# A gated graph network on one core: the update gate next to the reset gate in the first of a round's six steps

## The reference

```
h = relu(layernorm(x));  q, k, v = h@Wq.T, h@Wk.T, h@Wv.T
rel = adj.T * (q@k.T);   rel /= norm(rel, axis=2);   x = x + rel@v
h = relu(layernorm(x))
repeat 3 times:
    a = adj@h (used as a_in and as a_out);  av = [a, a]
    z = sigmoid(av@w3.T + b3 + h@u3.T + bu3)
    r = sigmoid(av@w4.T + b4 + h@u3.T + bu3)
    c = tanh  (av@w5.T + b5 + (r*h)@u5.T + bu5)
    h = (1-z)*h + z*c
x = x + h
```

## Time and profile before

| | |
|---|---|
| median of 3 runs | 1028.66 us (1027.58 to 1029.11) |
| span of the profiled execution | 1027.9 us (no device time of its own is listed for it) |
| PE busy | 990.2 us, 96% |
| DVE busy | 773.5 us, 75% |
| ACT busy | 596.1 us, 58% |
| POOL busy | 87.3 us, 8% |
| mean granted TensorE clock | 0.991 |

### The profile page before, as it was taken

How to read it: one execution, slowest core, us unless ns; L and a number is a source line. 1 busy time by engine, 2 the same in 40 slices (tenths; PEclk the granted TensorE clock), 3 DMA queues, 4 the chain that set the end, 5 groups by cost and what they waited for, 6 DMA issues and landing times.

```text
span 1027.9 us, 16089 instructions
## 1 busy us (share of the span) xinstructions
PE 990.2 (96%) x5448; PEld 852.0 (83%) x5448; DVE 773.5 (75%) x1519; ACT 596.1 (58%) x1050; POOL 87.3 (8%) x90
## 2 busy tenths in 40 slices
PE   5799999999999999999999999999999999999996
PEld 4778888888888888878888788887888888888885
DVE  4877768778687777877778776877868777687765
ACT  4546665566656575665656556556564566655562
POOL 1110001001011010100001000100001000010000
PEclk9799999999999999999999999999999999999999
DMA  5010000200001000100002000010000100000001
GB/s 160 2 41 1 1 1 21 63 0 0 0 20 62 0 0 0 58 25 0 0 0 82 1 0 0 20 62 0 0 0 20 62 0 0 0 20 21 1 2 41
DMA packets 21409, 20.32 MB, mean 20 GB/s; under 512 B 2160, under 2 KB 21360, under 8 KB 21360
## 3 DMA queue, kind: packets, MB, share of 16 engines
q1 hardware_dynamic: 21360, 19.83, 6.1%
HBM read 11.44 MB, written 8.39 MB: 19 GB/s over the span
## 4 chain that ended last, share of the span: by engine, by line
PE 88%; DVE 5%; issue 3%; ACT 3%; DMA 1%; DVEq 0%; SPq 0%; POOL 0%; ACTq 0%
PE gate L304 12%; PE gate L306 11%; PE gate L305 11%; PE cand L304 8%; PE cand L306 8%; PE cand L305 8%; PE tok L395 3%; PE fea L405 3%; PE tok L405 3%; PE tok L304 2%; PE tok L306 2%; PE tok L305 2%; PE fea L360 2%; PE fea L304 1%; PE fea L306 1%
## 5 line engine op out<-in xcount | busy, mean ns | idle before, releaser
L854 DVE TENSOR_TENSOR d_s<-c_s,h 128x512 f32<-128x512 f32 x96 | 64.2, 688 | 58.6 <-ACT c_s L694 43.7
L675 ACT ACTIVATE r_s<-gate,b_r 128x512 f32<-128x512 f32 x96 | 64.2, 684 | 75.3 <-PE gate L306 75.3
L597 ACT ACTIVATE h_hi<-h 128x512 fp32r<-128x512 f32 x64 | 39.5, 632 | 98.6 <-DVE h L991 98.6
L264 POOL TENSOR_TENSOR rstd<-vare,minus_half 128x4 f32<-128x4 f32 x32 | 38.2, 1194 | 517.1 <-DVE vare L882 517.1
L304 PE MATMUL gate<-a_hi,W_hi_wz 128*128 128x512 f32 x192 | 79.3, 413 | 0.4
L597 ACT ACTIVATE a_hi<-a_s 128x512 fp32r<-128x512 f32 x96 | 60.5, 630 | 31.6 <-DVE a_s L958 31.1
L694 ACT ACTIVATE c_s<-cand,b_c 128x512 f32<-128x512 f32 x96 | 64.7, 682 | 22.8 <-PE cand L306 20.8
L304 PE MATMUL cand<-a_hi,W_hi_w 128*128 128x512 f32 x192 | 77.9, 406 | 0.0
L304 PE MATMUL cand<-rh_hi,W_hi_u 128*128 128x512 f32 x192 | 77.5, 404 | 0.0
L304 PE MATMUL gate<-h_hi,W_hi_u 128*128 128x512 f32 x192 | 76.3, 397 | 0.0
L305 PE MATMUL gate<-h_lo,W_hi_u 128*128 128x512 f32 x192 | 75.5, 393 | 0.0
(11 more groups left out here) (129 smaller groups left out, 2709.8 us busy)
## 6 DMA issues: line engine op xcount, KB each, us to landing
x_s<-x SPq DMA_DIRECT2D x16, 512.0 KB, 4.8
out<-o_s SPq DMA_DIRECT2D x16, 512.0 KB, 3.0
z_s<-w_t SPq DMA_DIRECT2D x1, 512.0 KB, 4.1
r_s<-w_t SPq DMA_DIRECT2D x1, 512.0 KB, 4.9
c_s<-w_t SPq DMA_DIRECT2D x1, 512.0 KB, 5.9
rh<-u_t SPq DMA_DIRECT2D x2, 256.0 KB, 6.2
d_s<-wq SPq DMA_DIRECT2D x1, 256.0 KB, 3.8
d_s<-wk SPq DMA_DIRECT2D x1, 256.0 KB, 4.6
```

The lines of the kernel that those rows point to most:

```text
L264: nc.gpsimd.tensor_tensor(rstd[n][:], vare[n][:], minus_half[:], ALU.pow).then_inc(rstd_ready[n], 1)
L597: return nc.scalar.activation(dst, src, ACT.Copy)
L675: nc.scalar.activation(r_s[:, c, :], gate[:, c, :], ACT.Sigmoid, bias=b_r[:, c:c + 1]).then_inc(r_ready, 1)
L854: return nc.vector.tensor_tensor(dst, a, b, ALU.subtract)
```

## The change

Only the order of work in window 1 changes, on three engines. On PE the update gate comes directly behind the reset gate, then the transposes, then `candidate_a`, and then both adjacency products next to each other. On ACT the reset sigmoid comes ahead of the state's copies, and the copy of r*h ahead of that of the transposed state. On DVE the low half of r*h comes ahead of the first adjacency sum (and so ahead of `shifts`). No instruction is added or removed.

```diff
@@ tensor, window, k == 1
                     reset_gate(w, s)
+                    update_gate(w, s)
                     transpose_state(w, o, use("step 1"))
-                    update_gate(w, s)
+                    candidate_a(w, s)
                     pe.wait_ge(tok_taken, 2 * use("step 1") + 2)
                     adjacency(w + 1, 0, feaA, use("adj 1"))
-                    candidate_a(w, s)
                     adjacency(w + 1, 1, tokA, use("adj' 1"))
                     candidate_rh(w, s)
@@ scalar, window, k == 1
+                    reset_sigmoid(w)
                     split_state(w, o)
-                    reset_sigmoid(w)
+                    split_rh(w)
                     split_tok(use("step 1"))
                     update_sigmoid(w)
                     take_a_aside(0, feaA, use("adj 1"))
-                    split_rh(w)
                     if attention:
                         normalise(0, 2 * i + 2, 0)
                     take_a_aside(1, tokA, use("adj' 1"))
```

## The result

The changed kernel takes 1040.67 us (median of 4, 1040.32 to 1041.73) against 1028.80 in the same comparison: ratio 1.0118, 95% interval 1.0104 to 1.0132. It is slower by 1.2%, as forecast (1039 us, range 1031 to 1044). One disturbed execution of a kernel further down (1114.15 us, at a mean granted clock of 0.847) is left out of all figures.

A forecast was written before the change was run, and what follows sets the result against it. PE, busy 990.2 of 1027.9 us, was taken to bound the kernel. Six rounds at +1.4 (8.4), +1.6 in the first and +0.1 behind the loop make +10.1, so 1039 us, range 1031 to 1044.

The forecast's parts named there:

- The pause that goes: Window 1, PE behind the reset gate: two pauses, 1.33 us together, vanish; with 0.14 of change-overs a gift of 1.47 us each round.
- The chain behind it: Window 1, ACT and DVE: later copies put `candidate_rh` 0.25 us later than before and `transpose_hx` 1.56 us late.
- What comes back in window 2: PE's existing 0.68 us wait for `a_s` shrinks, so 1.4 us a round stays of 1.56; bounds 0.25 and 1.56.
- The sum: Whole program: 8.4 us for rounds 2 to 7, 1.6 first round, 0.1 behind the loop: +10.1, median 1039 us.
- ACT's own turn of the loop: ACT's loop top: a costlier turn makes the second sigmoid 0.63 us later, +3.8 more, 1042.6 us; chance 0.08.
- that rival: PE's clock: window 1's two pauses bring half clock for 6.5 us each round, +23, 1062 us; chance 0.07.
- Faster: Window 1: DVE doesn't bind, PE keeps its 1.47 us a round, -10.3, 1018.4 us; chance 0.06.
- little changes: Window 1: `candidate_rh` waits as forecast, the wait ahead of `transpose_hx` is hidden, +0.25 x 7, 1030.4 us; chance 0.09.
- a granted clock under 0.99: Sign on PE's clock, listed among those that would show the prediction wrong.

The follow-up runs named there:

- one swap ahead of each wait: Against the changed kernel, separately: r*h ahead of `h_lo` on DVE, 1031.31 us; second `take_a_aside` ahead of the layer norm (`hx`) on ACT, 1032.12 us.
- both with the shifts: Changed kernel with r*h ahead of `h_lo`, second `take_a_aside` ahead of `hx`, and `shifts` ahead of `sum_a(0)`: 1023.05 us, ratio 0.9935.
- two kernels: PE's new order alone on the kernel before, 1061.41 us; ACT's and DVE's new lists alone, with PE's list as before, 1052.41 us.
- a third: Changed kernel with `rh_lo` ahead of the layer norm statistics on DVE: 1048.92 us, ratio 1.0200.

## Why the prediction was right

**The pause that goes.** Right. The update gate starts 5.44 us into the round, at the place forecast; the sigmoid of the second half ends at 201.61 and was wanted at 202.08.

**The chain behind it.** The forecast was a list of start times, which can be laid beside the rows (both in us from the round's start):

| step | forecast | measured |
|---|---|---|
| ACT `h_hi` | 6.21 | 6.23 |
| DVE r*h | 8.07 | 8.10 |
| DVE `t_lo` | 10.52 | 10.57 |
| PE first adjacency | 11.96 | 12.23 |
| DVE `rh_lo` | 13.87 | 13.82 |
| PE `candidate_rh` | 15.31 | 15.25 |
| DVE `sum_a(1)` | 18.57 | 18.51 |
| PE `transpose_hx` | 19.41 | 19.25 |

One hand-over was mis-sized. The first adjacency product was forecast 0.15 behind DVE's last `t_lo`, a figure read from the transposes; it starts 0.37 behind it (207.14 to 207.51). This moved nothing behind it, since `candidate_rh` waits for `rh_lo` anyway, but it takes from that wait: between the end of the adjacency products and `candidate_rh` lie 1.15 us, not the 1.5 forecast, and ahead of `transpose_hx` 1.17, not 1.3 (the idle times shown, 0.99 and 1.01, with the overlap of 0.16 added).

That this chain is the cause, and not only the order in which things are seen, is shown by two runs: one swap ahead of each wait takes that wait away, the first but for 0.35 (-1.15 and -1.16 us a round), and both with the shifts turn the loss into a gain.

**What comes back in window 2.** This step was wrong in its mechanism, and that 1.4 came near 1.50 was luck. I took 1.4 of the 1.56 and said that PE's existing wait for `a_s` would shrink. It didn't: it is 0.68 as before. The rows of before show why it could not:

```profile
226.04 0.60 ACT L597 ACTIVATE a_aside<-fea 128x512 f32<-128x512 f32 x1 [2.90 <-PE fea L407]
226.78 0.69 DVE L958 TENSOR_TENSOR a_s<-fea,a_aside 128x512 f32<-128x512 f32 x1 [0.22 <-ACT a_aside L597]
```

And those of the changed kernel:

```profile
227.28 0.28 PE L405 MATMUL fea<-adjT_s,t_hi 128*128 128x256 f32 x1
228.35 0.60 ACT L597 ACTIVATE a_aside<-fea 128x512 f32<-128x512 f32 x1 [2.86 <-PE fea L407]
229.08 0.69 DVE L958 TENSOR_TENSOR a_s<-fea,a_aside 128x512 f32<-128x512 f32 x1
```

This `a_s` is the sum over PE's own adjacency product a moment earlier. ACT stands idle for that product, DVE follows ACT, and PE waits for DVE, so the whole trip moves with PE: from the start of the product to the scores it takes 2.64 us in both kernels (224.97 to 227.61, 227.28 to 229.92). A late PE can take nothing out of it. The delay at `transpose_hx` was smaller than forecast (1.40, not 1.56), and window 2 gave nothing back but added 0.09, which is 1.49 at the scores and 1.50 a round. The transposes that come out of a wait take 0.85 and not 0.80, and the 36 matmuls behind them 8.30 and not 8.26, which makes up the 0.09.

**The sum.** The span grew by 10.8, with +10.1 forecast: 1.6 in the first round (forecast 1.6) and 8.9 in the six others up to the seventh `transpose_hx` (forecast 8.4); the prologue, which the change doesn't touch, was 0.8 shorter in this execution; +0.5 from there to the last transposes (forecast 0.1); and +0.6 behind their start, of which below. The step from span to median was mis-sized as well. I read the 0.76 between the profiled span and the median as what lies around a span. In all later runs of before, which list both figures, it is 1.74 to 1.85 us, so the profiled execution of before was about 1 us longer than the median one. This makes up some 1 us of the 1.7 by which the median missed.

**The rivals.** ACT's own turn of the loop doesn't show: its first sigmoid starts 3.39 us after its last operation, waiting for PE and not for itself. The clock was granted at 1.00 in all seven rounds of the changed kernel, so that rival didn't come true here, but its mechanism is real, and near: pauses of about 2 us instead of 1 brought it into two kernels, and pauses of 2.8 us into a third. Faster and little changes are refuted by the rows above; the time of the little case came with one swap (1031.31 and 1032.12), a gain with three. The prediction also named a granted clock under 0.99 as a sign of being wrong. Three of the four executions had 0.988, but so did some of the kernel before (0.988 to 0.992), so that sign could tell nothing.

## What to carry to other kernels

When an operation is moved ahead on one engine, look at what stands behind it there, and at what the other engines have queued behind its result: here r*h needed only the sigmoid, yet stood behind an operation that needed the copy the sigmoid had pushed back. A wait in the old trace is slack only if its chain starts somewhere else: where it starts at the waiting engine's own work, it moves along and gives nothing back. Reorder the lists of all engines as one schedule; here each half alone lost more than the whole, and the whole gained only after three more swaps. A forecast of this kind can be made by laying start times end to end from the old trace, at the pitch of pairs and not at the length of single operations.

## What the hardware showed

The clock reacts to pauses near the size of those that a small reordering makes. Two waits of about 1.0 us in each round left it at 1.00; behind a wait of 1.99 us it was at 0.51 for 3.4 us, while in three other rounds of that execution it stayed at 1.00 behind waits of 1.92 to 2.12; in one kernel it fell behind a wait of 2.75 in one round and stayed at 1.00 behind one of 2.82 in another. The executions of that last kernel vary by several us (1046.82 to 1054.12). Their mean clocks of 0.988, 0.984 and 0.980 go with 1046.90, 1050.95 and 1054.12 us, but the fastest of all had 0.938, so the link is likely and not shown.

The program's last eight transposes follow the same wait of 3.91 us in both kernels, and lasted 1.09 us before and 1.97 us in the changed kernel:

```profile
1032.55 1.97 PE L395 MATMUL tok<-ident,h 128*128 128x128 f32 x8 [3.91 <-DVE h L991]
```

That nearly 1 us at the end is a matter of the execution, not of the change: it was 1.64 to 1.97 in eight of the nine experiments, with PE's list of before among them, and 1.09 in the ninth.
